# A six-stage transformer kernel on one core: input in four transfers, both attentions' first chunks and ends rearranged, and part of the first attention's masks added by VectorE

## What is computed

```python
x = x + 0.5 * _L0_ffn_ref(_layernorm(x), ...)   # F0a: 2 shared and 8 experts of 256, top 2, silu-gated
x = x + _L0_attn_ref(_layernorm(x), ...)        # A0: 16 heads of 8, band |i - j| <= w // 2
x = x + 0.5 * _L0_ffn_ref(_layernorm(x), ...)   # F0b
x = x + 0.5 * _L1_ffn_ref(_layernorm(x), ...)   # F1a: 8 experts of 512, top 2 with capacity, squared relu
x = x + _L1_attn_ref(_layernorm(x), ...)        # A1: 16 heads of 8, hyperbolic distance, full 512 x 512
x = x + 0.5 * _L1_ffn_ref(_layernorm(x), ...)   # F1b
```

```python
fluct = jnp.abs(x[:, -1] - x[:, -2])
a = jax.nn.sigmoid(alpha)
signal = a * fluct.mean() + (1.0 - a) * fluct[0, 0]
w = jnp.floor(24 + (120 - 24) * jax.nn.sigmoid(signal)).astype(jnp.int32)
scores = jnp.where(abs(i - j) <= w // 2, scores, -1e+30)
```

## Time and profile before

| what | value |
|---|---|
| median of 3 runs | 3094.23 us (3093.03 to 3098.08) |
| the profiled execution | 3093.71 us |
| its span, first to last instruction | 3092.0 us |
| its mean granted TensorE clock | 0.862 of full speed |
| busy share over the span | PE 84%, DVE 75%, ACT 71%, POOL 53% |
| load phase | 0 to 51 us |
| first attention | 419 to 827 us |
| second attention | 1601 to 2706 us |

### The profile page before, as it was taken

How to read it: one execution, slowest core, us unless ns; L and a number is a source line. 1 busy time by engine, 2 the same in 40 slices (tenths; PEclk the granted TensorE clock), 3 DMA queues, 4 the chain that set the end, 5 groups by cost and what they waited for, 6 DMA issues and landing times. The chain is left out here.

```text
span 3092.0 us, 42285 instructions
## 1 busy us (share of the span) xinstructions
PE 2596.8 (84%) x12174; PEld 1727.2 (56%) x12208; DVE 2308.9 (75%) x4325; ACT 2207.5 (71%) x2470; POOL 1652.8 (53%) x1312
## 2 busy tenths in 40 slices
PE   5999959999799996999965778777787777579998
PEld 4877845666487784878752223223233332258887
DVE  5677646677467667889968778787787877398887
ACT  3555525566455554777746999999999999667776
POOL 2676652222176664454445576666766767434444
PEclk9999979999899998999986676676766767689999
DMA  3111102222111112111100000000000000021111
GB/s 118 55 41 54 41 11 52 50 48 48 46 49 48 41 54 83 42 55 41 54 0 1 0 1 1 0 1 1 1 1 1 1 1 1 0 111 45 52 47 48
DMA packets 26068, 103.77 MB, mean 34 GB/s; under 512 B 6336, under 2 KB 8384, under 8 KB 16704
## 3 DMA queue, kind: packets, MB, share of 16 engines
q1 hardware_dynamic: 25920, 102.01, 9.7%
HBM read 82.33 MB, written 2.62 MB: 27 GB/s over the span
## 5 line engine op out<-in xcount | busy, mean ns | idle before, releaser
L1792 POOL TENSOR_TENSOR A_Y<-A_Y,A_U 128x2048 f32<-128x2048 f32 x86 | 390.0, 4559 | 226.4 <-ACT A_U L1835 226.4
L1868 DVE TENSOR_SCALAR A_U<-ps 128x1024 f32<-128x1024 f32 x256 | 308.9, 1217 | 127.4 <-POOL A_Y L1792 63.6
L1874 DVE SCALAR_TENSOR_TENSOR A_U<-ps,A_U 128x1024 f32<-128x1024 f32 x256 | 310.8, 1214 | 54.8 <-PE ps L2004 54.8
L2004 PE MATMUL ps<-A_QT,A_KT 9*128 9x512 f32 x512 | 181.6, 706 | 196.8 <-DVE A_U L1874 164.0
L478 POOL TENSOR_TENSOR F0b_h<-F0b_h,dn 128x512 f32<-128x512 f32 x128 | 212.0, 1661 | 112.4 <-DVE F0b_h L410 112.2
L478 POOL TENSOR_TENSOR F0a_h<-F0a_h,dn 128x512 f32<-128x512 f32 x128 | 212.1, 1662 | 104.9 <-DVE F0a_h L410 104.8
L2004 PEld LDWEIGHTS ps<-A_QT,A_KT 9*128 9x128 f32 x512 | 66.0, 254 | 333.1 <-DVE A_U L1874 244.3
L1792 POOL TENSOR_TENSOR dn<-dn,A_U 128x2048 f32<-128x2048 f32 x42 | 190.3, 4553 | 111.8 <-ACT A_U L1835 111.8
L1835 ACT ACTIVATE A_U<-A_U 128x2048 f32<-128x2048 f32 (+1 forms) x96 | 236.5, 2464 | 0.0
L1976 PE MATMUL ps<-A_Y,A_VA 128*32 128x512 f32 x688 | 226.9, 793 | 5.8 <-DVE A_OT L1774 3.0
L1311 DVE CUSTOM_DVE_ANT_0 ps<-ps,A_mask 128x256 f32<-128x256 f32 (+1 forms) x512 | 184.6, 421 | 61.9 <-PE ps L1383 61.0
(11 more groups left out here) (372 smaller groups left out, 8121.5 us busy)
## 6 DMA issues: line engine op xcount, KB each, us to landing
dn<-weight_rows SPq DMA_DIRECT2D x32, 1024.0 KB, 4.6
F1a_cwb<-weight_rows SPq DMA_DIRECT2D x16, 1024.0 KB, 4.6
F1b_cwb<-weight_rows SPq DMA_DIRECT2D x16, 1024.0 KB, 4.7
A_KZ<-A_KT SPq DMA_DIRECT2D x132, 64.0 KB, 2.0
A_QZ<-A_qs SPq DMA_DIRECT2D x96, 64.0 KB, 2.0
dn<-in_down SPq DMA_DIRECT2D x2, 2048.0 KB, 12.3
stage<-in_up SPq DMA_DIRECT2D x1, 2560.0 KB, 8.8
X<-in_x SPq DMA_DIRECT2D x1, 2048.0 KB, 8.4
```

The lines of the kernel that those rows point to most:

```text
L1792: eng.tensor_tensor(flat(y_slot(m, h)), flat(y_slot(m, h)), flat(Um[:, h % UR]), ALU.add).then_inc(s["t_ready"], 1)
L1868: eng.tensor_scalar(u_step(n), d_pair(n), 0.0, None, ALU.max).then_inc(s["dp_vector"], 1)
L1874: eng.scalar_tensor_tensor(out=u, in0=g_pair(), scalar=CLAMP, in1=u, op0=ALU.min, op1=ALU.mult).then_inc(s["u_ready"], 1)
L2004: last = eng.matmul(ps[:, 4 + b, :], KT[r:r + 9, pair, kt * P:(kt + 1) * P], QT[r:r + 9, pair, :], start=True, stop=True)
```

## The change

1. Load phase: x comes in four transfers with a semaphore each. The router's weights, the up and the down weights follow on SyncE; 24 small transfers are issued by ScalarE. VectorE puts the statistics of chunk c+1 ahead of the normalisation of chunk c. The upper and lower parts of the up weights are made in four parts, ScalarE's between its copies. ScalarE clears A0's QA, KA and VA there (in the other four chunks), and VectorE makes A0's distance table. These tiles get a place that outlives the phase.
2. A0, start: keys are projected, taken and assembled before queries; the mask is made behind both; GpSimd clears only KZ ahead of the rows and QZ behind them.
3. A0, padding transfers of keys carry 24 rows in place of 32, and the wait for them moves into `scores`.
4. A0, masks: for the tiles 0 and 3 and the half 0 TensorE leaves the mask matmul out, and VectorE adds the mask to the finished scores in PSUM (`mask_scores`) before ScalarE's exponential.
5. A0 and A1, end: the four turns go to banks 0 to 3 one after the other, and the divisions use a reciprocal tile each. In A1 VectorE applies the last layer norm and ScalarE makes the copies of it.
6. A1, start: squares by ScalarE, sums, reciprocal and assembly by VectorE, the eight side columns by GpSimd beside it. Four turns come before the first step, twelve inside the first burst, two a step; ScalarE copies the turns 1, 3 and 4 to 11.
7. Semaphores of the feed-forward phases are merged (`top_made`, `rest_made`), with the same order of work.

The diff, cut to its core:

```diff
@@ load phase, SyncE
-                    eng.dma_start(X[:, :, :], x).then_inc(load["x"], 16)
...
+                    for i in range(PARTS):
+                        tiles = slice(i * TILES // PARTS, (i + 1) * TILES // PARTS)
+                        eng.dma_start(X[:, tiles, :], x[:, tiles, :]).then_inc(x_in[i], 16)
+                    eng.dma_start(rw[0][:, :], router0).then_inc(load["router"], 16)
                     eng.dma_start(stage[:, :], up0).then_inc(load["up0"], 16)
                     eng.dma_start(dn0[:, :, :, :], down0).then_inc(load["rest"], 16)
+                    for dst, src in ((qkv_w[0], w_qkv0), (qkv_w[1], w_qkv1), (out_w[1], wo1)):
+                        eng.dma_start(dst[:, :], src).then_inc(load["small"], 16)
@@ load phase, ScalarE (24 transfers ahead of this loop)
                     for c in range(B):
                         eng.wait_ge(s["tr_done"], c + 1)
                         eng.activation(XT[:, c * S:(c + 1) * S], ps[:, c % 6, :], ACT.Copy).then_inc(s["xt_copied"], 1)
+                        if 2 <= c < 2 + PARTS:
+                            if c == 2:
+                                eng.wait_ge(load["up0"], 16)
+                            cols = slice((c - 2) * part, (c - 1) * part)
+                            eng.activation(up0_hi[:, :, :].rearrange("p u n -> p (u n)")[:, cols], stage[:, cols],
+                                           ACT.Copy).then_inc(s["split_done"], 1)
+                        else:
+                            for n in range(2 * (c % 4), 2 * (c % 4) + 2):
+                                flat, lo = cleared[n]
+                                eng.activation(flat[:, lo:lo + 1024], zero[:, :].to_broadcast([P, 1024]), ACT.Copy)
@@ load phase, VectorE
+                    stats(0)
                     for c in range(B):
+                        if c + 1 < B:
+                            stats(c + 1)
                         eng.wait_ge(s["rstd_ready"], c + 1)
@@ A0, GpSimd
-                        eng.memset(QA[:, :, :, :, :].rearrange("p c t h r -> p (c t h r)").bitcast(F32), 0.0)
-                        eng.memset(KA[:, :, :, :].rearrange("p t h r -> p (t h r)").bitcast(F32), 0.0)
-                        eng.memset(VA[:, :, :, :].rearrange("p t h r -> p (t h r)"), 0.0)
...
+                        eng.memset(KZ[:, :, :, :].rearrange("p n j q -> p (n j q)").bitcast(F32), 0.0)
                         eng.drain().then_inc(pad_ready, 1)
...
                         eng.wait_ge(s["qs_ready"], 1)
+                        rows_k(0)
+                        eng.wait_ge(s["qs_ready"], 2)
                         rows_q(0, 0)
+                        eng.memset(QZ[:, :, :, :].rearrange("p n j q -> p (n j q)").bitcast(F32), 0.0)
+                        eng.drain().then_inc(pad_ready, 1)
@@ A0, SyncE
-                                eng.dma_start(KZ[r:r + 32, g % 2, j, :].bitcast(F32),
-                                              KT[r:r + 32, g, :].bitcast(F32)).then_inc(s["kz_ready"], 16)
+                                eng.dma_start(KZ[r:r + 3 * HD, g % 2, j, :].bitcast(F32),
+                                              KT[r:r + 3 * HD, g, :].bitcast(F32)).then_inc(s["kz_ready"], 16)
...
+                                if not done and g == 1:
+                                    eng.wait_ge(pad_ready, 2)
@@ A0, ScalarE
-                                eng.wait_ge(s["s2_done"], 2 * n + i + 1)
+                                if by_vector(m, i):
+                                    eng.wait_ge(s["masked"], masked_by(c, u))
+                                else:
+                                    eng.wait_ge(s["s2_done"], 2 * n + i + 1)
@@ A0, VectorE
+                        def mask_scores(c, u):
+                            m = u % 4
+                            if not by_vector(m, 0):
+                                return
+                            _, _, w0, w1 = window(m)
+                            eng.wait_ge(s["s2_done"], 2 * (UNITS * c + u) + 1)
+                            eng.tensor_tensor(two(4, w0, w1), two(4, w0, w1),
+                                              mask[:, w0:w1].unsqueeze(1).to_broadcast([P, 2, w1 - w0]),
+                                              ALU.add).then_inc(s["masked"], 1)
...
                                 maxima(c, p, n)
+                                u = n - BEHIND
+                                if u >= 0:
+                                    mask_scores(c, u)
+                                elif not first:
+                                    mask_scores(c - 1, u + UNITS)
@@ A0, TensorE
+                                if not by_vector(m, i):
+                                    eng.matmul(two(4 + i, w0, w1), ident_b[:, :],
+                                               mask_b[:, :].rearrange("p (b w) -> p b w", b=2)[:, :, w0:w1], start=True,
+                                               stop=False, skip_group_check=True)
                                 eng.matmul(two(4 + i, w0, w1), KT[:, g, m * P:(m + 1) * P],
+                                           QZ[:, g % 2, 2 * i:2 * i + 2, lo:hi], start=by_vector(m, i), stop=True,
@@ A0 and A1, TensorE, end
-                            turn_out(eng, B, t)
+                            for g in range(4):
+                                last = eng.transpose(ps[:, t, g * P:(g + 1) * P], OT[:, g, t * P:(t + 1) * P], ident[:, :])
+                            last.then_inc(s["on_tr"], 1)
@@ A1, VectorE, end
-                        add_back_vector(eng, B, B - 1)
-                        copy_norm_vector(eng, B)
...
+                        norm_stats_vector(eng, s, B, B - 1)
+                        norm_apply_vector(eng, s, B, B - 1)
@@ A1, TensorE and ScalarE, first chunk
+                                if first and i < 6:
+                                    for n in (4 + 2 * i, 5 + 2 * i):
+                                        eng.wait_ge(s["turned"], n - 1)
+                                        turn_tensor(eng, 0, n, first_bank(n))
...
+                            if first:
+                                first_squares_scalar(eng)
+                                for i in (1, 3):
+                                    turned_scalar(eng, i, first_bank(i))
+                                for i in range(4, 12):
+                                    turned_scalar(eng, i, first_bank(i))
@@ A1, VectorE, first chunk (first_rows_vector)
+                    eng.wait_ge(s["s_ready"], 1)
+                    eng.tensor_scalar(KA[:, :, 0:32].rearrange("p h (a r) -> p h a r", a=2)[:, :, :, 0:HD],
+                                      k3.unsqueeze(2).to_broadcast([P, TPC * H, 2, HD]), -2.0, None, ALU.mult)
...
+                    assemble(eng)
+                    eng.wait_ge(s["sides_ready"], 1)
+                    eng.sem_inc(s["asm_done"], 1)
```

More of the change, by code:

```diff
@@ L71, in macaron @@
         col = sb("col", [P, 24])
[L74 to L77, removed]
+        load = {k: sem(f"load_{k}") for k in ("router", "up0", "up1", "rest", "small", "dn1")}
+        top_made, rest_made, restart_ready = sem("top_made"), sem("rest_made"), sem("restart_ready")
+        TOPS, RESTS = (0, 2, 4, 7), (0, 1, 2, 4)
         weights_out = sem("weights_out")
@@ L789, in _ @@
                         if c == 1:
-                            eng.wait_ge(load["small"], 16 * (12 + H))
+                            eng.wait_ge(load["router"], 16)
                         if c > 0:
@@ L797, in _ @@
                     last.then_inc(s["lg_done"], 1)
+                    eng.wait_ge(load["small"], 16 * (11 + H))
                     eng.matmul(ps[:, 6, 0:D], wo_t[:, :], wfc[:, :], start=True, stop=True).then_inc(step, 1)
@@ L816, in _, with stats @@
                 def _(eng):
-                    eng.wait_ge(load["x"], 16)
-                    for c in range(B):
+                    def stats(c):
+                        if c % (B // PARTS) == 0:
+                            eng.wait_ge(x_in[c * PARTS // B], 16)
                         tiles = range(TPC * c, TPC * (c + 1))
@@ L1008, in spreads, with by_vector, masked_by @@
                     return 64 * k
+                def by_vector(m, i):
+                    return i == 0 and m in (0, 3)
+                def masked_by(c, u):
+                    return 2 * (TPC * c + u // 4) + (u % 4) // 3 + 1
                 def older(c):
@@ L1296, in take_k, with mask_of_columns @@
                                               ALU.add).then_inc(s["qs_ready"], 1)
+                        def mask_of_columns():
+                            eng.wait_ge(step, n0 + 4)
+                            eng.tensor_scalar(col[:, 18:19], col[:, 22:23], 1.0, None, ALU.add)
+                            eng.drain()
+                            eng.reciprocal(col[:, 19:20], col[:, 18:19])
+                            eng.drain()
+                            eng.tensor_scalar(col[:, 21:22], col[:, 19:20], 96.0, 24.0, ALU.mult, ALU.add)
```

(26 more changed lines are left out.)

300 lines of the change are left out of this document (189 added, 111 removed).

## The result

The kernel after takes 3043.08 us (median of four runs, 3042.67 to 3046.86); before, run beside it, took 3095.33 (3093.03 to 3098.08). The ratio is 0.9834, 95% interval 0.9817 to 0.9851: 52 us faster. The forecast was 3039 in 3028 to 3056, so it lay 4 us low. The profiled execution is the slowest of the four (3046.86 us, span 3045.1). Its parts are compared with the profile of before, 3092.0.

A forecast was written before the change was run, and what follows sets the result against it. TensorE was taken to bound the first attention, ScalarE the second, with serial starts and ends; gains 17.5 + 13.5 + 5 + 2 + 12 + 5.5 = 55.5 us from 3094.2 give 3039, range 3028 to 3056.

The forecast's parts named there:

- Load stage: First phase: statistics ahead of normalisation and x in quarters end it at 32.7 us for 50.4; 17.5 us gained, 11 to 19.
- 2 + 6.4/4 = 3.6 us is what I take: first data at 4.5 us: Load phase: about 2 us fixed plus a quarter of the rest for x's first transfer, so first data at 4.5 us.
- Rival (b): Load phase: x lands as one, so the phase gives 13 us, or 12 with dearer issues; 3044 us, chance 0.12.
- Start of the first attention: Before the first scores: fewer clears and keys first let scores start 13.5 us earlier, 11 if queries were last.
- Masks: First attention: 64 mask matmuls left out gain 6.4 us, less 1.6 for waits: 5 gained, bounds +11 and -6.
- rival (a): First attention: VectorE's additions eat the gain as TensorE waits, -6 us for +5; 3050 us, chance 0.25.
- I count 0.10: First attention: TensorE gains 0.10 us per mask matmul left out, not 0.17, as weight loads are no longer hidden; 6.4 us.
- 0.2 us a chunk: First attention: added waits of TensorE where VectorE already lags, 0.2 us in each chunk, 1.6 us in all.
- A0's end: End of the first attention: turns and divisions over four banks gain 2.7 us, less 0.6 for additions: 2, 1 to 3.
- A1's end: End of the second attention: turns 2.7 us, normalisation moved to VectorE 2.3, higher clock 0.5: 5.5 gained, 4.5 to 6.
- A1's start: Start of the second attention: first relu 13.4 us sooner, first burst 20 to 24 us for 21.6; 12 gained, 8 to 14.
- rival (c): Second attention's first burst: ScalarE's copies and TensorE's turns alternate over two banks, giving back 7 us; 3046 us, chance 0.13.

The follow-up runs named there:

- joined pair: Kernel after with x in 1, 2, 2, 3 chunks, small transfers on SyncE, 32-row key padding, ScalarE copying last four turns: 3039.41 us without additions, 3041.78 with 64.

## Why the prediction was right, and where not

**Load stage: right, 1.5 us too much.** (The prediction's own 50.4 - 32.7 is 17.7, not 17.5.) The failed step is "2 + 6.4/4 = 3.6 us is what I take: first data at 4.5 us". They came at 6.25. The transfers of ScalarE issued beside x cost 1.42 of the 1.75. With these gone it still landed 0.33 late, beside the other quarters. Rival (b) did not come: one transfer lands 3.6 us later than the quarter. Nor did the four follow each other at 2 us apiece: the last landed at 10.70, where the prediction allowed for 15.

**Start of the first attention: right** in sum (13.23 for 13.5) and in each step. "24 rows nothing" was wrong by 0.67.

**Masks: wrong in sign.** The forecast counted 6.4 gained and 1.6 lost. The whole first attention with 64 additions and 24 rows took 393.89, 393.18, 391.79, 392.07, 394.12 and 393.43 us in six profiles, 393.1 in the mean; without, 391.50. So the masks cost about 1.6 us by these, and 2.4 by the medians of the joined pair, whose ranges overlap, where the term said 5 gained and rival (a) 6 lost: the rival's mechanism, at about a third of its size.

Two steps failed. The first is the price of the steady chunks, "I count 0.10" for a mask and "0.2 us a chunk" for VectorE's lag. From TensorE's turn of the output in the first chunk to that in the seventh lie six chunk periods. Here they are with x as one transfer, which has the additions, and with no addition, both at full clock on one chip (start:end, length, then busy of PE, PEld, DVE, ACT and POOL, clock), each with TensorE's wait for the maxima:

```profile
498.09:757.56 259.47, 253.44 (x1945) 161.82 (x1968) 205.22 (x965) 155.17 (x318) 55.78 (x84) 1.00 0.19 43
PE ps L1462 <- DVE A_QA L1362: 5.0, 8, 1.5
```

```profile
498.02:756.65 258.63, 255.72 (x1993) 164.04 (x2016) 185.28 (x918) 158.61 (x319) 55.92 (x84) 1.00 0.19 43
PE ps L1461 <- DVE A_QA L1361: 2.6, 4, 0.9
```

TensorE is busy 2.28 us less for 48 masks, 0.05 each in place of 0.10, and waits 2.4 us more for VectorE's maxima, 0.4 a chunk in place of 0.2. (The 6.9 us of the earlier trace rows are those of TensorE's weight loads; its matmuls waited 5.5 us for the maxima.) The two cancel: the period was 43.2 to 43.4 us in the six profiles with additions and 43.1 to 43.5 in the three without (before is one of them, at 43.35).

The second is the tail, for which the forecast had 0.6 for additions (under the ends) and nothing for the clock. From the end of TensorE's last wait for a padding transfer of queries to the last turns pass 7.9 us in the three profiles without additions. With 64 additions it is 8.8 where the clock held and 11.8 to 11.9 where it fell for 6.8 us behind such a wait of 1.3. (TensorE waits 2.1 us for exponentials in the last 24 us, and without additions for none.) This is the kernel after, from 8.1 us ahead of the end of that wait:

```profile
762.00:772.00 10.00, 7.98 (x67) 3.75 (x66) 4.23 (x16) 6.64 (x16) 1.02 (x1) 1.00 0.12 28
772.00:779.00 7.00, 7.00 (x35) 3.76 (x33) 0.19 (x1) 2.93 (x6) 0.00 (x0) 0.51 0.00 0
```

and this the same piece of work with unequal transfers:

```profile
760.57:770.57 10.00, 7.88 (x65) 3.75 (x66) 4.24 (x16) 6.61 (x16) 1.02 (x1) 1.00 0.12 28
770.57:777.57 7.00, 5.55 (x51) 2.81 (x51) 0.76 (x2) 4.08 (x9) 0.00 (x0) 1.00 0.00 0
```

0.51 is the 1.2 GHz level. In the 10 us before it fell TensorE had been busy 7.98; where it held, 7.88, and the wait in them was 1.32 and 1.34 us. So the work just ahead doesn't tell the two apart. The fall costs 3 us. Of the six profiles it came in four, mean 393.7 for the whole attention, and not in two, 391.9. It came in three of the other four with additions, and not in that with 128 of them; it never came in the three without (before, no addition, joined). Three are few, so that additions make the fall likelier is what the runs suggest and no more. What decides it from execution to execution is open.

**A0's end: right, too small.** 3.18 for the 2.7 of turns and divisions. Of the rest, 13.85 us from the last division to F0b became 12.31: in before the granted clock was 0.50 behind the divisions, here 0.67. The 0.6 for drained additions belongs to the stretch ahead, and is counted there.

**A1's end: right, 1.7 too small.** Turns 3.1, the projection up to the root 1.4, the normalisation 2.2, small ones 0.5. The 0.5 for the clock should have been 1.4.

**A1's start: right, 3 us too much.** The relu came 12.0 earlier, 1.4 under the forecast's 13.4, and the burst took 24.54, just above "20 to 24". The burst gave back 2.9 us, as rival (c) had it, at less than half of its 7. Of its mechanism the runs show TensorE's matmuls coming later than VectorE wants them, 3.4 us of waits for 0.9. They don't show the half clock as the cause: the burst was as long at a granted clock of 0.58 as at 0.74. The part "two copies each" on VectorE was worth 0.4 to 1.4.

**Sum.** By the profile the forecast was 1.5 too high in the load stage, 8.3 in the stretch of the masks, 3.0 in A1's start and 1.0 in its chunks, 0.3 in A0's start, and 2.7 and 1.7 too low in the ends and 1.1 in phases that didn't change. That is 8.6, the 55.5 forecast against 46.9. The profiled execution was the slowest; by the medians 52.3 were gained, 3.3 less than forecast. The range held because the errors of the terms had both signs; that part of the agreement is luck.

**Signs of being wrong.** ScalarE's issues ended at 11.6 us, under the 15; the first burst took 24.5, under the 27; the chunk period stood at 43.4 for 43.35, so it didn't fall to "42.9 to 43.3". The first square root came 11.4 us sooner for 12.

## What to carry to other kernels

Where a serial chain begins with a load, the first transfer is sized for the first step alone, the next one so that it lands before that step ends, and nothing that isn't wanted soon is issued beside them, by any engine. Moving a matmul off the engine that sets the pace pays only if what takes its place is not in a chain: here an addition of 0.59 us came between scores and exponential, and over six chunks the 2.3 us that TensorE was spared came back as 3.1 us of idle time. Two profiles of a stretch are compared from the same piece of work, not from the same distance to its end. Serial starts and ends are where a trace foretells best: each gave its gain within 3 us.

## What was not expected of the hardware

A transfer of 24 rows and 48 KB was issued in 0.77 us and one of 32 rows and 64 KB in 0.60 (3.08 and 2.41 for four), and the smaller one landed no sooner: from the last of the first four issues to the first scores pass 2.23 us for 2.16. The first quarter of x, 512 KB, took 5.4 us from issue to landing with three more quarters and ScalarE's small transfers in flight, and 4.0 without the small ones, where 2048 KB alone took 8.4 in before. And one program with the same waits in its tail ran seven microseconds of it at 2.4 GHz in one execution and at 1.2 in another, after the same work.
